# A two-layer transformer kernel: layer 0's opening in another order, layer 1's score rows in a block, and the short key tile on all 128 columns

## The reference

```python
x = _layernorm(x + _L0_attn_ref(x, ...))   # causal softmax attention, 16 key heads
x = _layernorm(x + _L0_ffn_ref(x, ...))    # silu(up) * gate, weights rounded to -1, 0, 1 times a scale
x = _layernorm(x + _L1_attn_ref(x, ...))   # 4 key heads, slope * -|i - j| added to the scores
x = _layernorm(x + _L1_ffn_ref(x, ...))    # silu(gate) * up

# inside _L1_attn_ref: tokens near each other, and the first 64, are what is NOT attended to
qk = qk + alibi_slopes(H)[None, :, None, None] * dist[None, None, :, :]
qk = jnp.where(allowed[None, None, :, :], -1000000000.0, qk)
attn = jax.nn.softmax(qk, axis=-1)
```

## Time and profile before

| | |
|---|---|
| median of 3 runs | 1095.2 us |
| profiled execution: its own time | 1093.62 us |
| its span | 1091.9 us |
| TensorE busy | 992.9 us (91%) |
| VectorE busy | 699.2 us (64%) |
| ScalarE busy | 606.6 us (56%) |
| GpSimd busy | 348.0 us (32%) |
| mean granted TensorE clock | 0.976 |

### The profile page before, as it was taken

How to read it: one execution, slowest core, us unless ns; L and a number is a source line. 1 busy time by engine, 2 the same in 40 slices (tenths; PEclk the granted TensorE clock), 3 DMA queues, 4 the chain that set the end, 5 groups by cost and what they waited for, 6 DMA issues and landing times. The chain is left out here.

```text
span 1091.9 us, 18023 instructions
## 1 busy us (share of the span) xinstructions
PE 992.9 (91%) x6546; PEld 518.2 (47%) x6546; DVE 699.2 (64%) x1535; ACT 606.6 (56%) x1204; POOL 348.0 (32%) x418
## 2 busy tenths in 40 slices
PE   6587999999989899978799999999999989899997
PEld 4342323333324578755333343433333334588996
DVE  2766877777753457569788777787777735235323
ACT  4334667666766433462467667777777676523221
POOL 3022122231111335341343453614233251424323
PEclk9798999999999899999899999999999999999999
DMA  7443011121000020042443140303121000000001
GB/s 261 160 145 98 16 46 59 59 60 50 11 2 1 18 71 1 8 121 89 141 107 112 52 148 16 125 2 125 34 92 37 1 2 1 1 1 20 20 1 39
DMA packets 32996, 64.20 MB, mean 59 GB/s; under 512 B 6095, under 2 KB 22367, under 8 KB 30532
## 3 DMA queue, kind: packets, MB, share of 16 engines
q1 hardware_dynamic: 31564, 58.47, 17.1%
q0 software_dynamic: 1072, 3.80, 1.0%
q10 hardware_dynamic: 272, 0.79, 0.2%
HBM read 50.45 MB, written 12.32 MB: 57 GB/s over the span
## 5 line engine op out<-in xcount | busy, mean ns | idle before, releaser
L1020 ACT ACTIVATE prob<-ps 128x512 f32<-128x512 f32 (+6 forms) x896 | 442.9, 537 | 208.8 <-PE ps L1063 201.2
L1063 PE MATMUL ps<-qop,kop 98*128 98x512 bf16 (+15 forms) x1376 | 302.6, 291 | 21.5 <-ACT prob L1020 7.9
L1049 PE MATMUL ps<-kop,qop 96*128 96x512 bf16 (+3 forms) x896 | 254.5, 358 | 37.9 <-DVE maxes L955 32.2
L1063 PEld LDWEIGHTS ps<-qop,kop 107*128 107x128 bf16 (+2 forms) x1376 | 114.5, 98 | 279.1 <-ACT prob L1020 200.8
L1090 PE MATMUL ps<-prob,vst 128*32 128x512 f32 (+4 forms) x1792 | 211.8, 544 | 3.9 <-POOL prob L892 2.6
L955 DVE CUSTOM_DVE_ANT_0 sums<-ps,tri 128x128 bf16<-128x128 f32 (+7 forms) x256 | 184.1, 755 | 47.1 <-PE ps L1049 45.8
L955 DVE CUSTOM_DVE_ANT_0 sums<-ps,table 128x960 bf16<-128x960 f32 x128 | 148.0, 1156 | 71.2 <-PE ps L1049 56.3
L892 POOL TENSOR_TENSOR prob<-prob,keep 128x384 int32<-128x384 int32 (+2 forms) x144 | 122.6, 853 | 221.7 <-ACT prob L1020 219.2
L1486 PE MATMUL ps<-xs,wffn 128*128 128x512 f32 x640 | 156.5, 400 | 3.7 <-PEq L730 2.2
L955 DVE CUSTOM_DVE_ANT_0 tri<-ps,table 128x960 bf16<-128x960 f32 x128 | 147.5, 1152 | 3.3 <-PE ps L1049 3.3
L1486 PEld LDWEIGHTS ps<-xs,wffn 128*128 128x128 f32 x640 | 120.7, 191 | 30.7 <-issue 4.2
(11 more groups left out here) (103 smaller groups left out, 687.5 us busy)
## 6 DMA issues: line engine op xcount, KB each, us to landing
table<-in_table SPq DMA_DIRECT2D x32, 464.0 KB, 4.7
qop<-q_parts SPq DMA_DIRECT2D x96, 128.0 KB, 2.7
kop<-k_parts SPq DMA_DIRECT2D x48, 128.0 KB, 2.6
kop<-k_parts SPq DMA_DIRECT2D x48, 96.0 KB
q_parts<-qop SPq DMA_DIRECT2D x8, 384.0 KB, 3.0
q_parts<-kop SPq DMA_DIRECT2D x8, 384.0 KB, 2.6
x<-in_x SPq DMA_DIRECT2D x4, 512.0 KB, 5.8
k_parts<-qop SPq DMA_DIRECT2D x4, 384.0 KB, 4.5
```

The lines of the kernel that those rows point to most:

```text
L1020: nc.scalar.activation(prob[0:rows, q % 2, k % HG, lo % CH:lo % CH + hi - lo], ps[0:rows, t_bank(n, k), lo % CH:lo % CH + hi - lo], ACT.Ex ...
L1049: last = nc.tensor.matmul(ps[:, S_BANK + 2 * (k % S_SLOTS) + a // CH, a % CH:a % CH + b - a], qop[0:RD, par, h, i0:i0 + P], kop[0:RD, par, ...
L1063: return nc.tensor.matmul(ps[0:rows, bank, a % CH:a % CH + b - a], lhs, rhs, start=start, stop=True, skip_group_check=True)
```

## The change

Four things, all in the order or the layout of the work. The amount of arithmetic stays the same, except that the matmuls of the short key tile write 128 partitions instead of 64.

1. In `plan`, for layer 1 and groups from 1 on, no unit stands behind a quad's first exponent row; all that are due stand behind the second.
2. In layer 0's opening the `finish` of a unit stands behind the next unit; the last one of sequence 0 goes over into the part beside the maxima.
3. Beside layer 0's maxima all steps count the same and are spread by the count of units, not by TensorE time and width.
4. The matmuls of the key tile kt = 7 take 128 stationary columns; the upper 64 of them are the first keys of the next version in `kop`. For that the three versions change places (`kpos` likewise), so that the one that lies last is never used with this tile. ScalarE still reads 64 partitions.

```diff
@@ -132,6 +132,12 @@
     stream_next = [(k, 2) for k in range(lead)] if group + 2 < N else []
     late, last = group >= 1, group == N - 1
     steps, given, given_next = [], 0, 0
+
+    def behind(h, done, due):
+        if layer.index == 1 and late:
+            return done if h == 0 else due
+        return done + -(-(due - done) // (HG - h))
+
     tail = [("values", nq - 1), ("evict", 1), ("norm", 1)]
     for n, (half, kt) in enumerate(quads):
         due = min(len(stream), -(-len(stream) * (n + 1) // rows_at))
@@ -140,10 +146,10 @@
             steps.append(("parts", 0, 1))
         for h in range(HG):
             steps.append(("exp", HG * n + h, 0))
-            upto = given + -(-(due - given) // (HG - h))
+            upto = behind(h, given, due)
             steps += [("max", u, later) for u, later in stream[given:upto]]
             given = upto
-            upto = given_next + -(-(due_next - given_next) // (HG - h))
+            upto = behind(h, given_next, due_next)
             steps += [("max", u, later) for u, later in stream_next[given_next:upto]]
             given_next = upto
         if n == 0 and late:
@@ -172,7 +178,7 @@
     return steps
 
 
-PE_SHARE = {"turn": 0.85, "unit": 1.72, "v": 1.72}
+PE_SHARE = ({"turn": 1, "unit": 1, "v": 1}, {"turn": 0.85, "unit": 1.72, "v": 1.72})
 
 
 def opening_of(layer, proj):
@@ -180,7 +186,7 @@
 
 
     units = units_of(layer)
-    behind = [step if len(step) == 3 else (*step, PE_SHARE.get(step[0], 0.0)) for step in proj.beside_maxima()]
+    behind = [step if len(step) == 3 else (*step, PE_SHARE[layer.index].get(step[0], 0.0)) for step in proj.beside_maxima()]
     out = []
     if layer.index == 0:
 
@@ -192,11 +198,13 @@
         first += [("ternary", 1), ("ternary", 2)]
         out = [(what, k, 0) for what, k in first]
 
-    width = [hi - lo for _, _, lo, hi in units]
+    width = [hi - lo for _, _, lo, hi in units] if layer.index == 1 else [1] * len(units)
     work, given, at = sum(share for _, _, share in behind), 0.0, 0
     for n in range(len(units)):
         out.append(("max", n, 1))
         due = work * sum(width[:n + 1]) / sum(width[:-2])
+        if layer.index == 0:
+            due = -(-work * (n + 1) // (len(units) - 2))
         while at < len(behind) and given + behind[at][2] <= due + 1e-6:
             given += behind[at][2]
             out.append((*behind[at][:2], 0))
@@ -340,9 +348,10 @@
             vs = [("v", v) for v in range(b * 4, b * 4 + 4)]
             out = [*turns]
             for j in range(4):
-                one, two = units[2 * j:2 * j + 2]
-                out += [one, two, ("finish", one[1]), vs[j], ("finish", two[1])]
-            return out
+                for _, u in units[2 * j:2 * j + 2]:
+                    out += [("unit", u), ("finish", u - 1)] if u >= 1 else [("unit", u)]
+                out.append(vs[j])
+            return out if b == 0 else out + [("finish", len(self.units) - 1)]
         u, t, f = units, turns, [("finish", k) for _, k in units]
         return [*t[:4], u[0], u[1], f[0], ("weigh", 3), ("decay", 3), u[2], f[1], *t[4:6], f[2], ("divide", 3), ("scale", 3),
                 u[3], *t[6:], f[3], u[4], u[5], f[4], ("v", 1), f[5]]
@@ -350,7 +359,7 @@
     def beside_maxima(self):
 
         if self.i == 0:
-            return self.steps(1)
+            return [*self.steps(1)[:-1], ("finish", len(self.units) - 1, 1)]
         first, second = self.steps(1)[:2], self.steps(1)[2:]
         downs = [("down", k, 1.75 if k < CT else 0.6) for k in range(2 * CT)]
         return [*downs[:CT + 2], ("second", 0), *downs[CT + 2:], ("second", 1), ("root", 0), ("root", 1), *first,
@@ -655,7 +664,7 @@
 
         L, kop, kpos = self.L, self.K.kop, self.dram.kpos
         sp.dma_start(kop[L.score_rows:L.rows, buf, :, :],
-                     kpos[NPOS - 2:NPOS, 1:2, :].to_broadcast((2, L.key_sets, T))).then_inc(self.const_rows[buf], 16)
+                     kpos[NPOS - 2:NPOS, 0:1, :].to_broadcast((2, L.key_sets, T))).then_inc(self.const_rows[buf], 16)
         if L.index == 1:
             sp.dma_start(kop[L.dot_rows:L.score_rows, buf, :, :], kpos).then_inc(self.const_rows[buf], 16)
 
@@ -1056,20 +1065,22 @@
                 half, kt = quads[k // HG]
                 h = k % HG
                 lo, hi = columns_of(L, half, kt)
-                j0, rows = key_tile(L, kt)
+                j0, _ = key_tile(L, kt)
                 q = qop[0:RA, par, h, :]
 
                 def mm(a, b, lhs, rhs, start):
-                    return nc.tensor.matmul(ps[0:rows, bank, a % CH:a % CH + b - a], lhs, rhs, start=start,
+                    return nc.tensor.matmul(ps[:, bank, a % CH:a % CH + b - a], lhs, rhs, start=start,
                                             stop=True, skip_group_check=True)
 
                 if i == 0:
                     return mm(lo, hi, kop[0:RA, par, h, j0:j0 + P], q[:, lo:hi], True)
                 start = True
-                for v, a, b in ((1, 0, j0 + WIN), (2, j0 + WIN, j0 + 3 * WIN), (0, j0 + 3 * WIN, T)):
+                for v, a, b in ((0, 0, j0 + WIN), (1, j0 + WIN, j0 + 3 * WIN), (2, j0 + 3 * WIN, T)):
                     a, b = max(a, lo), min(b, hi)
                     if a < b:
-                        last = mm(a, b, kop[0:RA, par, v, j0:j0 + rows], q[:, a:b], start)
+
+                        sets = kop[0:RA, par, :, :].rearrange("p v t -> p (v t)")
+                        last = mm(a, b, sets[:, v * T + j0:v * T + j0 + P], q[:, a:b], start)
                         start = False
                 return last
 
@@ -1690,7 +1701,7 @@
     high, low, unit = (pos // P * P).astype(np.float32), (pos % P).astype(np.float32), np.ones(T, np.float32)
     left = np.stack([high] * 3 + [low] * 3 + [unit] * 3)
     mixed = np.where(((pos - GLOB) // GLOB) % 2 == 0, 1.0, -1.0).astype(np.float32)
-    kpos = np.stack([left, -left, left * mixed], axis=1)
+    kpos = np.stack([-left, left * mixed, left], axis=1)
 
     slopes = np.float32(2.0 ** (-(2.0 ** -(np.log2(H) - 3.0)))) ** np.arange(1, H + 1, dtype=np.float32)
     s = three_parts(slopes)
```

## The result

| | before | changed |
|---|---|---|
| median of the runs, us | 1094.7 (1093.52 to 1096.86, 4 runs) | 1076.24 (1074.84 to 1077.8, 4 runs) |
| ratio on one chip | | 0.9829, interval 0.9809 to 0.985 |
| profiled execution, us | 1093.6 | 1076.21 |
| its span, us | 1091.9 | 1074.4 |
| start of layer 0's first exponent row | 92.24 | 87.31 |

18.5 us faster, where 14.8 were forecast (1080.4). Of the span's 17.5 us, 4.9 are there at layer 0's first exponent row, 6.0 at layer 1's, and 11.4 more come within layer 1's attention; nothing comes behind it.

A forecast was written before the change was run, and what follows sets the result against it. TensorE was taken to bound the kernel, with waits for ScalarE in layer 1 and VectorE in layer 0's opening. 1093.6 - 10.4 - 4.4 = 1078.8, beside the median 1080.4; own range 1077.5 to 1083.5, whole range 1076 to 1088.

The forecast's parts named there:

- ScalarE's second exponent: Layer 1's quads, groups 1 to 6: two exponent rows ahead of score rows save 0.10 or 0.08 us each, 6.3 us.
- The change of column count: Layer 1's quads 7 and 15: 128 columns everywhere save 0.24 us each, 3.1 us, plus 1.0 from earlier exponents.
- Layer 1 together: Layer 1's attention: 6.3 + 3.1 + 1.0 = 10.4 us off; bounds 3.1 and 19.3.
- Layer 0's opening: Layer 0's first maxima: earlier start and fewer waits between TensorE and VectorE, 4.4 us off; bounds 1.0 and 7.0.
- the two walks: Step-by-step timings of layer 0's maxima in present and new order, ending at 89.0 and 84.6 us.
- all behind it (...) moves along: Behind layer 0's maxima: the row of maxima, its DMA and the first exponent row come earlier by the same 4.4 us.
- rival D: Opening escapes the low clock, or the half-clock stretch behind the first exponents meets less work: 3 to 4 better, 1077; 0.08.
- the step from the execution to the median: Whole kernel: the profiled execution lay 1.6 us under the median of 1095.2, so forecast 1078.8 became 1080.4.
- A: Layer 0's opening: half clock runs on to 62.5 and the opening's gain is gone, 1085.2 us; chance 0.15.
- B: Layer 1: the fourth exponent row doesn't wait for the exponents' distance; only 3.1 and 4.4 come, 1087.7 us; chance 0.14.
- C: Layer 1: the second score row waits for VectorE's slot in each of 93 quads; 1121 us at 0.7 delay; chance 0.05.
- estimate from the Trainium skill's page TensorEngine Tiling (Array Packing): Layer 1's short key tile: widening would double about 4 x 0.2 us in 13 quads, +10 us instead of -3.1.

The follow-up runs named there:

- The block alone: Only layer 1's score rows stand together behind the second exponent row, short tile narrow, opening as before, against the kernel before: 1083.78 us, ratio 0.9897.

## Why the prediction came out as it did

**ScalarE's second exponent (forecast 6.3).** Right, place and size. 448 columns 2.78 to 2.68 (forecast 2.68), 512 columns 3.04 to 2.95 (forecast 2.95), quads 1 and 9 at nothing, the pair of exponentials 1.08 to 0.98; added up over the quads 6.5. The kernel with both Ms behind the first E, slower by 45 us with the same matmuls, shows that it is the position of the second E.

**The change of column count (3.1, and 1.0 with the exponents).** Right in mechanism and size: quad 7 lost 0.25 and quad 15 0.24 with the wide tile alone, 3.3 in all (2.5 by medians). With the block quad 7 lost 0.36 (forecast 0.34) and quad 15 0.33 (0.32). Two things were told too simply. The block alone removes half of the changes, so of the 3.3 only 2.0 are left for the wide tile beside it. And 0.24 is not the price of the four changes in a quad: in quad 7 the third row comes at 1.64 instead of 1.21, 0.43 late, and 0.18 of it is won back because TensorE then no longer waits for ScalarE ahead of the fourth row.

**Layer 1 together: 10.4 forecast, 11.4 measured.** By the starts of the quads in both traces: group 6's part with Ms gained 1.32 (forecast 1.26), groups 1 to 5 with quad 15 of group 0 9.24 (8.94), quad 7 of group 0 0.24 (0.24). These hold. Not in the terms were 0.45 in the first two quads of group 0 (8.51 before, 8.06 after), which is the chance of the half clock described above, and 0.15 behind group 6's last M, mostly group 7's short key tile. So the change gained 11.0 here, and 0.45 was luck.

**Layer 0's opening: 4.4 forecast, 6.2 measured over nine traces.** This is the step that failed, by its size: the term 89.0 - 84.6 = 4.4 us of the two walks. The walk takes 1.0 off the start of the maxima (47.1 to 46.1), 0.5 off the first head (11.0 to 10.5) and 2.9 off heads 2 to 4 (30.9 to 28.0). The last part is right: 31.15 to 28.16, gained 3.0. It is what runs at half clock that was mis-sized. As means of the four traces with the old opening and the five with the changed one, the start came 1.9 earlier (47.2 to 45.3) and the first head became 1.2 shorter (10.2 to 9.0), together 3.1 where the walk had 1.5. The first exponent row came 6.2 earlier (92.5 to 86.3). Both walks held the half clock until 52.2; by the granted clock in the traces it ended at 51.4 to 53.5 in the four and at 46.7 to 51.7 in the five. Why it ended earlier, and how much of the 1.6 comes from that, no run shows. By medians the opening is worth 6.8 (18.5 less the 11.7 of layer 1's parts) to 7.6 (alone).

The profiled pair shows less of this: 4.9 at the first exponent row, the start 1.2 earlier, the first head 0.7 shorter. It has another 1.1 between the first exponent rows of layer 0 and layer 1, where the prediction says "all behind it (...) moves along". TensorE has the half clock in a stretch around the first exponents, before and after:

```profile
92.24:100.00 7.76, 7.76 (x24) 2.65 (x28) 5.51 (x15) 4.29 (x8) 1.55 (x3) 0.50 0.63 187
```
```profile
87.31:92.60 5.29, 5.29 (x16) 2.04 (x17) 3.21 (x11) 3.37 (x7) 0.64 (x1) 0.50 0.59 158
```

Before, 7.76 us of exponent rows ran at half clock, after it 5.29: 2.5 less, worth 1.2 at the full clock. This is the half of rival D that had the stretch "behind the first exponents" fall on less work. But the change does not bring it about. From the first exponent row of layer 0 to that of layer 1 the four kernels with the old opening take 448.0 to 449.2 us and four with the changed one 447.6 to 449.6, with the same list there; the means, 448.5 and 448.2, are 0.3 apart. So the clause held, and the 1.1 are within the chance of the half clock.

**Sum.** 1093.6 - 14.8 = 1078.8 was the forecast of the profiled execution, which took 1076.21: 2.6 less, of which 0.5 lie before the first exponent row, 1.1 between it and layer 1's, 1.0 in layer 1's attention. The remaining 1.6 of the miss are the step from the execution to the median: before, the profiled execution was 1.6 under it, after, it lies on it (1076.21 and 1076.24). That step rested on three runs. The 35 later executions of the kernel before have medians of 1094.3 to 1094.8, so 0.4 to 0.9 of the 1.6 were a high median of the three.

**The rivals.** A (the low clock lasts) fell: it ended at 51.7, and earlier in the other four kernels with this opening. The half clock does not stand behind TensorE's idle 9 us of before, as the prediction has it, but begins within them, at 42.0 of 38.3 to 47.5. B (the fourth E isn't bound by the second exponential) fell by the quads and by the kernel with both Ms first. C (an M waits for VectorE's slot) fell in the changed kernel, where no such wait shows in the late groups, and holds in the three-unit quads of group 0, as it did before. D had two halves: that the second half-clock stretch falls on less work is true of this pair and no effect of the change; that the opening escapes the low clock is true in part in the five traces, and it is in that stretch that the opening's term fell short. The prediction's estimate from the Trainium skill's page TensorEngine Tiling (Array Packing) would have made the wide tile cost 10 us; the wide tile alone made the kernel 2.5 faster. The drain that its "Key Properties" tell of at a change of mode would fit the 0.11 us measured here at a change of column count; no run shows that a drain is what takes them.

**Chances.** Faster had 0.92 and came; by the prediction's own words (all but C and half of the rest) it adds up to 0.935. The time of 1076.24 lies below the likeliest case's own range (1077.5 to 1083.5) and only 0.24 above the lower end of the whole range (1076). The four runs, 1074.84 to 1077.8, lie on both sides of that end, so that the median is inside is luck. The lower end left no room for the forecast's own spread and rival D at once.

## What to carry to other kernels

Where two banks feed another engine, look whether both its inputs can stand ahead of any other matmuls: here the same four matmuls cost 45 us more one place earlier. Before costing a tile's width, look at the rows beside a change of column count; and when two edits remove the same change, price them together. A walk of the order was right to 0.1 us a head where the clock was full, and 1.6 us short in its gain where it was half: give such a stretch a width of its own in the range. And before a difference between two profiles is put down to a change, look at the same stretch in other kernels whose list is the same there: it told 3 us of order from 1 us of chance.

## What the runs showed that I had not expected

- A change between 64 and 128 output columns costs TensorE 0.11 us from a narrow row to a wide one (M at 0.50 instead of 0.39 behind two narrow rows) and 0.09 back (0.31 instead of 0.22 from the second matmul of an M to the next E, quad 7 before and with the wide tile). The weight load tells the two apart: the M's starts 0.01 behind the E's where both have 128 columns (712.09 and 712.08, before), and 0.30 behind it where the E has 64 (715.16 and 714.86). The narrow form itself is no faster (369 against 357 ns).
- ScalarE starts exponentials of 448 columns 0.44 apart where their inputs wait, though each is 0.545 long: a pair is 0.98.
- The stretches at half clock are between 3.4 and 13.7 us long, and their places and lengths differ between kernels with the same instructions in those places. The same kernel's runs differ by 0.5 to 5.5 us. Outside these stretches a kernel with the same list repeats closely: heads 2 to 4 within 0.01 us, layer 1's attention behind its first two quads within 0.1.
- An early start of the maxima and short maxima are not the same thing: the new finish order in sequence 0 gives an earlier start, and in sequence 1 it costs 1.0 us (heads 2 to 4 take 28.16 with it and 27.12 without).
